# Row-by-row tiles in a graph network's aggregations: every 22nd tile instead of every 33rd

## The reference

```python
# layer 0, three times; deg is the sum of edge weights plus 1
h = h @ W
out = segment_sum(h[src] * norm[:, None], dst)       # norm = dis[src] * ew * dis[dst]
z = relu(out + b)                                     # with self loops in src, dst
# layer 1
out = x + segment_sum(edge_weight[:, None] * x[src], dst)
out = relu(out @ W1 + b1) @ W2 + b2
# layer 2: attention over the edges (softmax by destination, three kinds of logits)
# layer 3
agg = segment_sum(x[src], dst) / max(deg, 1)
out = agg @ W_l.T + b_l + x @ W_r.T; out = out / max(norm(out), 1e-12)
```

## Time and profile before

| | |
|---|---|
| median of 3 runs (lowest, highest) | 6409.95 us (6406.93, 6410.04) |
| profiled execution | 6407.41 us, span 6405.7 us |
| mean granted TensorE clock | 0.704 of full speed |
| busy share: TensorE, VectorE, ScalarE, GpSimd | 60%, 49%, 17%, 72% |
| five passes (first gather to first gather of the next, where there is one) | 973.6, 972.0, 982.7 us, then the fourth and fifth with 953 us from first to last gather |
| the rest | setup 198 us, attention and its dense layers 4.1 to 5.4 ms |

### The profile page before, as it was taken

The page is one execution under the profiler, slowest core; times in us unless marked ns, Lnnn a source line. Parts: engine busy times, 40 slices in busy tenths (PEclk is TensorE's granted clock), DMA queues, the critical chain, the costliest instruction groups (busy, mean ns, idle before and its releaser), DMA issues.

```text
span 6405.7 us, 111135 instructions
## 1 busy us (share of the span) xinstructions
PE 3863.8 (60%) x19975; PEld 2756.6 (43%) x20158; DVE 3134.7 (49%) x8280; ACT 1109.1 (17%) x2896; POOL 4631.1 (72%) x4720
## 2 busy tenths in 40 slices
PE   1555555555555555555455555699999984555555
PEld 0433444433344444334333434556666663333345
DVE  7433333433333433333533333489999987223334
ACT  1100000000000000000100000277878773000001
POOL 9777777777777677777677777477777754777774
PEclk7666566666656655666566566899999996666667
DMA  2222222222222222222222222276676651222222
GB/s 68 79 55 55 55 55 55 73 55 55 55 55 55 68 55 55 55 55 55 64 55 55 55 55 55 66 153 155 153 153 153 153 121 36 55 55 55 55 55 56
DMA packets 411204, 468.73 MB, mean 73 GB/s; under 512 B 117250, under 2 KB 318293, under 8 KB 410530
## 3 DMA queue, kind: packets, MB, share of 16 engines
q0 software_dynamic: 150464, 307.83, 18.9%
q1 hardware_dynamic: 215124, 132.51, 9.2%
q10 hardware_dynamic: 44958, 21.26, 1.3%
HBM read 435.73 MB, written 27.81 MB: 72 GB/s over the span
## 4 chain that ended last, share of the span: by engine, by line
POOL 49%; issue 18%; PE 17%; DVE 9%; DMA 4%; ACTq 1%; ACT 1%; SPq 0%; DVEq 0%
POOL pool L886 48%; DMA pool<-table,src_col 4%; PE psum L1063 3%; PE psum L1141 3%; PE psum L1117 2%; PE psum L1099 2%; PE psum L1106 2%; PE psum L1028 1%; PE psum L1069 1%; PE psum L1092 1%; PE psum L1084 1%; DVE work L1961 1%; ACTq L516 1%; PE psum L1129 1%; ACTq L580 1%
## 5 line engine op out<-in xcount | busy, mean ns | idle before, releaser
L886 POOL DMA_INDIRECT pool<-table,src_col x3800 | 3608.6, 950 | 1237.3 <-issue 1121.7
L1063 PE MATMUL psum<-pool 128*128 x8300 | 1842.0, 392 | 2125.9 <-SPq L633 1512.4
L1063 PEld LDWEIGHTS psum<-pool 128*128 128x128 f32 x8300 | 1606.9, 283 | 2619.2 <-issue 2610.5
L1845 DVE TENSOR_TENSOR work<-work,psum 128x1024 f32 x520 | 634.7, 1221 | 3010.6 <-PE psum L1069 3007.8
L1855 DVE TENSOR_SCALAR pool<-iota_f,rel_col,ew_col 128x128 f32<-128x128 f32 x3320 | 893.1, 354 | 9.2 <-ACT work L1206 5.3
L858 POOL DMA_INDIRECT gath<-table,src_col x520 | 508.2, 977 | 188.8 <-issue 137.3
L1053 PE MATMUL psum<-zero_rows,iota_b 128*128 128x512 bf16 x1029 | 487.4, 571 | 13.0 <-DVE work L1845 9.1
L1069 PE MATMUL psum<-zero_rows,iota_b 128*128 128x512 bf16 x868 | 445.2, 593 | 34.1 <-issue 32.8
L1324 ACT ACTIVATE pool<-psum 128x512 f32<-128x512 f32 (+1 forms) x104 | 55.6, 562 | 1938.6 <-PE psum L1015 1936.5
L858 POOL DMA_INDIRECT ew_col<-table,src_col x312 | 299.5, 960 | 95.1 <-issue 94.8
L1324 ACT ACTIVATE pool<-psum,gcn_bias 128x512 f32<-128x512 f32 (+1 forms) x26 | 17.1, 658 | 1882.9 <-PE psum L1015 1882.9
(11 more groups left out here) (250 smaller groups left out, 3954.3 us busy)
## 6 DMA issues: line engine op xcount, KB each, us to landing
pool<-table SPq DMA_DIRECT2D x7040, 0.5 KB
pool<-table ACTq DMA_DIRECT2D x7040, 0.5 KB
pool<-table,src_col POOLq DMA_INDIRECT x3800
pool<-edge_attr SPq DMA_DIRECT2D x832, 64.0 KB
pool<-step_masks SPq DMA_DIRECT2D x624, 48.0 KB
pool<-rel_rows SPq DMA_DIRECT2D x208, 128.0 KB
table<-work ACTq DMA_DIRECT2D x48, 256.0 KB, 2.4
gath<-table,src_col POOLq DMA_INDIRECT x520
```

Of the source, the lines that this page charges most:

```text
L886: gp.indirect_dma_start(out=gath_ring[:, i % RING, :], out_offset=None, in_=source[:, :], in_offset=bass.IndirectOffsetOnAxis(ap=src_col[: ...
L1063: pe.matmul(window_sums(w)[:, bass.ds(places[s % REGS], 1), :].rearrange("p a d -> p (a d)"), hot_ring[:, s % HOT_RING, :], all_slots[:, b ...
L1845: v.tensor_tensor(into, into, window_sums(a), ALU.add).then_inc(steps.added, 1)
```

## The change

Every 22nd tile comes row by row: 34 row tiles (43, 65, ... 769) instead of 22, so 748 gathered tiles and 187 batches, 175 releases. The rows of a tile are no longer eight for each of 16 batches, but spread evenly over a window of batches: for SyncE from the place of its last row tile to that of this one (10 or 11 batches), for ScalarE the same, 9 batches earlier (AHEAD). Both now begin before the first batch. The semaphores for the rows are one for SyncE and two for ScalarE, cleared by SyncE after each row tile, in place of eleven that went on counting. ScalarE's release numbers get a row of `plan_reg` of their own, LAST_PAST, made in the setup by one more DMA, in which they lie side by side.

```diff
@@ -79,6 +79,7 @@
         PLAN = 6
+        LAST_PAST = PLAN + 1
@@ -153,7 +154,7 @@
-        EVERY = 33
+        EVERY = 22
@@ -161,13 +162,11 @@
-        ROW_BASE = 32
+        ROW_BASE = 64
         ROW_MAGIC = ceil_div(1 << 16, EVERY)
-        SPAN = 2 * (EVERY - 1) // BATCH
-        ROWS_PART = P // SPAN
-        BEFORE_RELEASE = SPAN // 2
+        ROW_LOAD = 16
+        AHEAD = 9
@@ -488,33 +487,35 @@
-        sync_rows = [sem(f"sync_rows{i}") for i in range(5)]
-        scalar_rows = [[sem(f"scalar_rows{i}{k}") for k in range(2)] for i in range(3)]
+        sync_rows = sem("sync_rows")
+        scalar_rows = [sem(f"scalar_rows{k}") for k in range(2)]
...
+        def rows_here(j):
+
+            return sync_rows if j % 2 == 0 else scalar_rows[j // 2 % 2]
+
+        def row_window(j):
+
+            ahead = AHEAD if j % 2 else 0
+            first = row_batch(j - 2) - ahead if j >= 2 else -1
+            return first, row_batch(j) - ahead
+
+        def fetch_rows(engine, kind, j, b, source, kept):
+
+            first, end = row_window(j)
+            lo, hi = (P * (x - first) // (end - first) for x in (b, b + 1))
             flat = source.rearrange("n d -> (n d)").bitcast(U8).rearrange("(a n) -> a n", a=1)
             into = all_slots[:, ROW_SLOT + j % ROW_SLOTS, :].bitcast(U8)
-            for k in range(ROWS_PART):
-                e = part * ROWS_PART + k
-                engine.dma_start(into[e:e + 1, :], flat[:, bass.ds(kept[part % 2 * ROWS_PART + k], D * 4)]
-                                 ).then_inc(rows_here(nth, j)[0], 16)
+            for e in range(lo, hi):
+                if e % ROW_LOAD == 0:
+                    kept[:] = nc.values_load_multi_w_load_instructions(
+                        plan_reg[ROW_BASE + j:ROW_BASE + j + 1, e:e + ROW_LOAD], engines=[kind], min_val=0,
+                        max_val=(N - 1) * D * 4, skip_runtime_bounds_check_because="sources are numbers of nodes")[1]
+                engine.dma_start(into[e:e + 1, :], flat[:, bass.ds(kept[e % ROW_LOAD], D * 4)]).then_inc(rows_here(j), 16)
@@ -595,22 +596,26 @@
-            act.wait_ge(past_loaded, 48)
+            act.wait_ge(past_loaded, 64)
...
+            def rows_after(b):
+                for u in range(1, NROW, 2):
+                    first, end = row_window(u)
+                    if first <= b < end:
+                        fetch_rows(act, mybir.EngineType.Activation, u, b, source, kept)
+
+            rows_after(-1)
             last = TILE_BATCHES - NBATCH
             for j in range(last):
                 if j % REGS == 0:
                     n = min(REGS, last - j)
-                    first = BATCH * j + BATCH - 1
-                    past = load_waits(mybir.EngineType.Activation, PLAN, first, (n - 1) * BATCH + 1, NW, BATCH)
+                    past = load_waits(mybir.EngineType.Activation, LAST_PAST, j, n, NW, 1)
                 act.wait_ge(steps.done, past[j % REGS])
                 act.sem_inc(slots_free, 1)
-                for u in range(1, NROW, 2):
-                    part = j - (row_batch(u) - SPAN - BEFORE_RELEASE)
-                    if 0 <= part < SPAN:
-                        fetch_rows(act, mybir.EngineType.Activation, steps.nth, u, part, source, kept)
+                rows_after(j)
@@ -625,18 +630,24 @@
+                def rows_after(b):
+                    for j in range(0, NROW, 2):
+                        first, end = row_window(j)
+                        if b == first and j >= ROW_SLOTS:
+                            sp.wait_ge(slots_free, steps.released(row_batch(j - ROW_SLOTS)))
+                        if first <= b < end:
+                            fetch_rows(sp, mybir.EngineType.SP, j, b, source, kept)
+
+                rows_after(-1)
                 for b in range(TILE_BATCHES):
                     sp.wait_ge(batch_here[b % NBATCH], batch_value(steps.nth, b))
                     for j in range(NROW):
                         if b == row_batch(j):
-                            sp.wait_ge(*rows_here(steps.nth, j))
+                            sp.wait_ge(rows_here(j), 16 * P)
+                            sp.sem_clear(rows_here(j))
                     sp.sem_inc(landed[steps.nth], 1)
...
+                    rows_after(b)
@@ -687,6 +698,9 @@
+            sp.wait_ge(past_loaded, 48)
+            sp.dma_start(plan_reg[LAST_PAST:LAST_PAST + 1, 0:NSW // BATCH], plan_reg[PLAN:PLAN + 1, BATCH - 1:NSW:BATCH],
+                         allow_slow_non_contiguous=True).then_inc(past_loaded, 16)
```

More of the change, by code:

```diff
@@ L163, in build @@
         ROW_SLOT = 84
-        ROW_BASE = 32
+        ROW_BASE = 64
         ROW_MAGIC = ceil_div(1 << 16, EVERY)
-        SPAN = 2 * (EVERY - 1) // BATCH
-        ROWS_PART = P // SPAN
-        BEFORE_RELEASE = SPAN // 2
-        assert (EVERY - 1) % BATCH == 0 and ROWS_PART * SPAN == P
-        assert all((t * ROW_MAGIC) >> 16 == t // EVERY for t in range(NT + 1))
+        ROW_LOAD = 16
+        AHEAD = 9
+        assert all((t * ROW_MAGIC) >> 16 == t // EVERY for t in range(NT + 1)) and ROW_BASE + NROW <= P
         assert all(sum(u < t for u in ROW_TILES) == max(t // EVERY - 1, 0) for t in range(NT))
```

## The result

| | before | after |
|---|---|---|
| median of 6 runs (lowest, highest) | 6408.61 us (6406.93, 6410.98) | 6809.65 us (6801.56, 6824.43) |
| profiled execution, span | 6407.41, 6405.7 us | 6824.21, 6822.4 us |
| mean granted TensorE clock | 0.704 | 0.687 |

The ratio is 1.063, with a 95% interval of 1.062 to 1.0641: the change makes the kernel 401 us slower. The direction was forecast, the size was not: 6625 us, with a range that ended at 6700.

A forecast was written before the change was run, and what follows sets the result against it. GpSimd's gathers bound the kernel before, ScalarE's queue after, at 968 us a pass plus an exposed tail. Passes of +49, +39, +46, +39 and +47 give +220 on 6407.4: 6627, rounded 6625 us, range 6500 to 6700.

The forecast's parts named there:

- rival (c): Release numbers load no faster (+28 us a pass), or the two busy row queues hinder each other: 6700 to 7000, 7%.
- 1, the gathers saved: GpSimd loses 12 gathers a pass, 60 in all: 75 us, if GpSimd still sets the pace.
- Rival (a): GpSimd still sets the pace, because ScalarE's loop has slack: 6332 us, 8%.
- 2, the price of a row: ScalarE and SyncE each issue 136 groups of 16 rows a pass at 6.6 us: 898 us.
- 3, the release loads: ScalarE's release numbers load in 1.22 us, not 3.755: 11 loads with their register work take 53 us a pass, not 81.
- 4, the releases: ScalarE's release waits themselves: 175 in a pass at 0.08 us, 14 us.
- 5, the order on ScalarE: ScalarE's loop takes 968 us a pass, nearly all ahead of GpSimd's last four gathers, all ahead of the dense copies.
- within 10 us: Sign: ScalarE's last row DMA of a pass comes this close to the last gather.
- 40 us of lag: GpSimd's ring of 12 batches takes up this much of ScalarE's lateness; then GpSimd waits for ScalarE.
- 6, the tail: The first dense copy of the second pass can't come before 968 us, then 43 us to the next pass: +39 us.
- some 45: Sign: us from the last gather to the next pass, not 21.
- 7, SyncE: SyncE's queue takes 945 us a pass at most, under ScalarE's 968, so it hides behind it.

The follow-up runs named there:

- sync_silent: The changed kernel, but SyncE issues none of its rows and waits for no even row tile; 8052.52 us, 0.9973 of the kernel before on its chip.
- every24: The changed kernel with every 24th tile row by row, 31 row tiles a pass; 8798.49 us, 1.0877 of the kernel before on its chip.
- every24b: The same kernel as every24, run on another chip; 8788.3 us, 1.0894 of the kernel before there.
- every256: The changed kernel with EVERY = 256, two row tiles a pass; 7692.71 us, 0.9449 of the kernel before on its chip.

## Why the prediction was right or wrong

The direction and the mechanism were right, and the size was not: the time lies where only rival (c) was to reach, which had 7%. By the steps:

**1, the gathers saved: right, and without effect, as forecast.** 748 gathers of 0.944 us, and GpSimd isn't the bound. Rival (a), 6332 us, fell. It was to hold only if 16 rows cost ScalarE under 6.3 us; they cost 6.84. The Trainium skill (DMA: Bandwidth & Descriptors, "Issuing engines are not separate DMA queues") calls the sequencer's time to start a DMA usually small beside the DMA itself. As a guide to the time of this kernel that doesn't hold: 40% of the chain are the starts of L518. Rival (c) had the right size and the wrong causes: the release loads did get shorter, and sync_silent leaves at most 0.09 of the 0.24 us below to queues that hinder each other.

**2, the price of a row: this is the step that failed.** The prediction read 6.6 us for 16 rows from one stretch of the kernel before. That is also its mean over all groups there, taken afterwards as above: 6.60 us on ScalarE, some 6.4 on SyncE. In the kernel after the same sum is 6.84 on ScalarE and 6.58 on SyncE. 136 groups x 0.24 = 33 us a pass, of the 36 by which the loop is longer than forecast (1004.4 against 968). With 6.84 the forecast's own sum is 136 x 6.84 + 54 + 14 + 3.5 = 1002 us. By the means, the load went from 1.20 to 1.31 us and the 16 DMAs together from 3.86 to 4.00, and the rest is in the gaps: some 15 us a pass for the load and 19 for the DMAs. The load's part follows from the change and could have been asked: every load of the row addresses that the prediction read stood behind a release, the diff shows that most no longer would, and the trace of before has no row of ScalarE's for the new place. The DMAs' part does not follow from the program alone: a group without a stall costs ScalarE 6.76 us in every24 and 6.88 in every24b, the same kernel, with DMAs of 224 and 231 ns. Within the first chip's runs it seems to have held still: 7 ns a row would be 76 us a run, and the six runs of the kernel after lie within 23. It was a mistake of mine to carry a unit price to the nearest percent over 136 groups and five passes and to allow only 16 us a pass above it. One tenth on a row, which the prediction priced at 90 us a pass and gave to rival (c), should have been in the range in part: 3.6% came true.

**3, the release loads: right in size.** 1.30 us, not 1.22, and 3.75 before: 1 us a pass off. **4, the releases: right.**

**5, the order on ScalarE: right in kind.** The last row is 0.4 us from the last gather ("within 10 us"), the loop never idles in mid-pass, and the first copy comes when the loop is through. Two details were off, both by the price. GpSimd's waits for the release were to be 30 us a pass and are 91.2 us in 70 waits, of which the usual 0.3 us gaps would have taken 21 anyway; by the forecast's step it is 1004 - 937 = 67. And none were to come in the first half, but the first over 0.4 us is at 1613.9, 346 us into the pass: at 6.84 a period of 42 gathers asks ScalarE for 58.8 us, not 56.9, so that 40 us of lag are reached after 340 us, not 500.

**6, the tail: nearly right.** 49.3 us from the first copy to the next pass, not 43. From the first copy to the last (2317.04) it is 44.9 us, not 38: the next copy behind the first comes only 8.6 us later, and two stages with a window take 8.3 us (2280.79 to 2289.11), not 7.6. The last 4.5 us were to be 4.8. From the last gather to the next pass it is 49.2 us, "some 45" in the forecast, and 21 before.

**7, SyncE: right that it hides, but it isn't free of ScalarE.** Its last row is at 2244.8, 977 us into the pass and 27 before ScalarE's. In the second pass I took the gap ahead of each of the 34 instructions of L647: before the 17 for its own rows it is 1.5 to 3.2 us, some 38 in all (17 x 2 in the forecast), and before those for ScalarE's rows at most 0.1 us until row tile 19, and from there on, but for one, 4.9, 5.1, 2.3, 3.0, 2.2, 8.0 and 13.9 us, 39 in all. So SyncE is held up by ScalarE's lag too, which no step of the forecast had, and that is why it is at 977 and not under 945: 136 x 6.58 + 13 + 38 + 39 = 985 us at most. With 27 us to spare behind ScalarE it sets nothing.

So the sum with the price of a row and the tail of the second pass as measured, 6627 + 5 x 33 + 5 x 6 = 6822 us, is the profiled time within 3 us. In part that is luck: what is left of a pass behind the 33 is 12.2, 9.7, 1.8, 6.5 and -0.5 us, not 6 each time. That the large term is the price of a row was worked out from the two traces, and that crowding isn't most of it from one experiment on another chip. It was not shown by an experiment on a chip where the kernel before takes 6409 us; nor was it tried there whether 24 or 28 instead of 22, with ScalarE's loop shorter than GpSimd's, would beat the kernel before. No kernel here beats both on both kinds of chip: every256 is the fastest of all on the experiments' chips, and would come out at about 6534 us on the first, by the estimate above.

## What to carry to other kernels

Before work is moved to an engine that looks idle, add up its queue and not its busy share: on ScalarE, at 17% busy, a row of 0.5 KB issued from a register held the queue for 0.43 us, and a pass had room for it only as long as the loop ended before the gathers. Price a unit that is multiplied by thousands at the place where it will stand in the queue, and with a margin of some per cent each way: the same load cost 1.22 us behind a release and 1.33 behind a row DMA, and the same DMA of the same program 224 ns in one run and 231 in another; and where an ordered queue has the next stage's work behind its loop, a late loop costs its lateness and the whole tail that used to be hidden. An aggregate wait names the last hand in a row of hands. On the first chip the engine whose next work waited only for "issue" was the late one, but "issue" alone isn't the sign (weight loads of TensorE, L1077, wait 2883 us for it in the kernel after without being late): the chain has to agree.

## What the runs showed of the hardware

The price of one instruction is not a constant of its form. The same 512-byte DMA on ScalarE's queue took 224, 228, 231, 232 or 235 ns by median in different runs, and 224 or 231 in two runs of one program. A load of 16 registers took ScalarE some 1.22 us right behind a semaphore instruction and 1.30 to 1.33 right behind a row DMA. A load of registers costs by count and stride: 1.30 us for 16 neighbours, 2.20 for 32, 3.74 for 16 that lie four apart.

On the first chip the queues of SyncE and ScalarE also pause for about 0.31 us once in every 128 of their instructions. That is the measure of queue 14's packets too: it has 572 of them in the kernel after, and the 73170 instructions of SyncE, ScalarE, VectorE and GpSimd in the trace are 572 times 128. In the second pass of the kernel after ScalarE has 38 such pauses, 12 us of its loop. They are in the price of a row given above, before and after.

The same program took 6409 us on one chip and 8077 to 8151 on four others, a quarter more, and the traces of those differ by stalls of the sequencers of SyncE, ScalarE and TensorE, at any instruction, of some 0.7 us and up to 1.4, and none on VectorE and GpSimd. What makes them stays open. A change that loads those queues is worth something else on each: +6.3% on the one, +10.8% on the other, with SyncE as the bound in place of ScalarE.
